# Two unread 512-column products at the turn of the second attention, and a new order of a few VectorE and ScalarE steps in the first attention and the feed-forward stages

## What is computed

```python
x = x + attn_a(layernorm(x), Wq, Wk, Wv, Wo)   # 16 heads of 16, masked softmax; 8 heads strided, 8 fixed
x = x + ffn(layernorm(x), w_gate, w_up, w_down) # 256 -> 704 -> 256
x = x + attn_b(layernorm(x), ...)               # 8 heads of 32
x = x + ffn(layernorm(x), ...)                  # the same weights again
```

```python
fid  = dots / (norm(qq) * norm(kq))            # a cosine, from 8 features per head
qw   = fid * (1.0 + 0.1 * sin(pi * fid))
aw   = 0.5 * qw + 0.5 * (Q @ K.T) / sqrt(32)
probs = softmax(aw); heads = probs @ V         # then Wo, a layernorm, a small middle net, a second layernorm
```

## Time and profile before

| | us |
|---|---|
| median of 3 runs | 3663.86 |
| lowest, highest | 3655.23, 3664.30 |
| the profiled execution, its own time | 3658.47 |
| its span | 3656.7 |
| mean granted clock of TensorE, share of full | 0.927 |

### The profile page before, as it was taken

How to read it: one execution, slowest core, us unless ns; L and a number is a source line. 1 busy time by engine, 2 the same in 40 slices (tenths; PEclk the granted TensorE clock), 3 DMA queues, 4 the chain that set the end, 5 groups by cost and what they waited for, 6 DMA issues and landing times. The chain is left out here.

```text
span 3656.7 us, 70567 instructions
## 1 busy us (share of the span) xinstructions
PE 3141.8 (86%) x24024; PEld 2441.3 (67%) x24024; DVE 2772.7 (76%) x7209; ACT 2187.4 (60%) x5360; POOL 1121.8 (31%) x664
## 2 busy tenths in 40 slices
PE   6899899899895899997588888888888886699998
PEld 4666666666664788887356565566665654688888
DVE  4676676676666788886488888888878887688887
ACT  4666667676672344433477777877777775344343
POOL 1000000000003455554233333444333333455554
PEclk9999999999996999999699999999999897899999
DMA  5344244244332100000334344443443443110000
GB/s 89 43 68 61 43 68 61 44 68 61 51 49 75 47 18 18 18 12 29 52 50 68 59 69 66 68 72 59 64 71 59 69 60 87 41 35 30 29 30 24
DMA packets 134183, 190.46 MB, mean 52 GB/s; under 512 B 15127, under 2 KB 81559, under 8 KB 133143
## 3 DMA queue, kind: packets, MB, share of 16 engines
q1 hardware_dynamic: 133830, 185.95, 29.9%
HBM read 45.65 MB, written 28.84 MB: 20 GB/s over the span
## 5 line engine op out<-in xcount | busy, mean ns | idle before, releaser
L407 ACT ACTIVATE a_probs<-a_probs,a_negmax 128x176 f32<-128x176 f32 (+4 forms) x1024 | 501.7, 490 | 331.6 <-DVE a_negmax L330 331.2
L330 DVE CUSTOM_DVE_ANT_0 a_probs<-a_mask,a_score 128x176 f32<-128x176 f32 (+4 forms) x1024 | 404.0, 400 | 222.4 <-PE a_score L481 90.2
L492 PE MATMUL a_turned<-ident,a_probs 128*128 128x128 f32 (+1 forms) x2176 | 427.7, 289 | 79.3 <-DVE a_pT L339 71.6
L1716 DVE CUSTOM_DVE_ANT_0 b_u<-b_u,b_score 128x512 f32<-128x512 f32 x512 | 340.4, 681 | 137.2 <-PE b_score L1971 134.8
L1841 ACT ACTIVATE b_u<-b_u,b_negmax 128x512 f32<-128x512 f32 x512 | 367.0, 717 | 113.6 <-DVE b_negmax L1716 112.2
L1245 PE MATMUL f_y_bank<-f_wdT,f_hqT 128*128 128x256 f32 x1536 | 374.7, 396 | 60.2 <-ACT f_hqT L1184 60.2
L1708 DVE SCALAR_TENSOR_TENSOR b_u<-b_u,b_score 128x1024 f32<-128x1024 f32 x256 | 310.1, 1215 | 94.2 <-ACT b_u L1834 91.7
L1245 PEld LDWEIGHTS f_y_bank<-f_wdT,f_hqT 128*128 128x128 f32 x1536 | 296.4, 197 | 108.5 <-issue 67.9
L1834 ACT ACTIVATE b_u<-b_score 128x1024 f32<-128x1024 f32 x256 | 262.3, 1025 | 163.3 <-PE b_score L1961 163.0
L1177 ACT ACTIVATE f_h_mag<-f_hu 128x704 f32<-128x704 f32 x128 | 101.4, 792 | 421.2 <-POOL f_hu L1060 421.2
L1980 PE MATMUL b_turned<-ident,b_u 128*128 128x128 f32 x2048 | 322.1, 282 | 24.7 <-DVE b_pT L1722 19.4
(11 more groups left out here) (236 smaller groups left out, 7160.5 us busy)
## 6 DMA issues: line engine op xcount, KB each, us to landing
b_stack<-b_part SPq DMA_DIRECT2D x192, 256.0 KB, 8.4
a_stack_q<-a_part SPq DMA_DIRECT2D x192, 128.0 KB, 4.3
a_stack_k<-a_part SPq DMA_DIRECT2D x192, 128.0 KB, 5.7
xs<-in_x_dram SPq DMA_DIRECT2D x16, 512.0 KB, 8.2
x_before_b<-xs SPq DMA_DIRECT2D x16, 512.0 KB, 2.9
b_xin<-x_before_b SPq DMA_DIRECT2D x16, 512.0 KB, 12.2
b_xres<-x_before_b SPq DMA_DIRECT2D x16, 512.0 KB, 3.8
x_after_b<-b_xres SPq DMA_DIRECT2D x16, 512.0 KB, 5.8
```

The source lines that it names most:

```text
L330: dve.tensor_tensor_reduce(out=probs[:, n % 2, j, 0:keys(n)], in0=mask_of(n), in1=score[j][:, 0:keys(n)], scale=-1.0, scalar=3.0e38, op0=A ...
L407: act.activation(probs[:, n % 2, j, 0:keys(n)], probs[:, n % 2, j, 0:keys(n)], ACT.Exp, bias=negmax[:, n, j:j + 1], scale=-1.0, accum_out= ...
L492: m = nc.tensor.transpose(turned[j % 2][0:rows, u, :], chunk(n, probs[:, n % 2, j, :], u), ident[:])
L1716: dve.tensor_tensor_reduce(out=u[:, n, j, :], in0=u[:, n, j, :], in1=score[:, j, :], scale=-0.05, scalar=3.0e38, op0=ALU.add, op1=ALU.min, ...
```

## The change

There are three edits, and no other.

1. First attention, VectorE: the side step of Q, K and R jobs moves from behind head 1 to behind head 2 (and its copy). V, y and input turns stay behind head 1, and ScalarE's order stays as it was.
2. Both feed-forward stages, ScalarE: `magnitude` moves behind `scalar_magnitude` (slot 0) and `scalar_standard` (slot 2).
3. Second attention, TensorE: `keep_busy` at (15, 1) and (15, 3), in the 16 bodies that have a next sequence: a product of the identity with 512 columns of a weight, written to the bank `out_acc`, which nobody reads before the next output product starts it anew.

```diff
-                        job = jobs.get(n - 1, "-") if j == 1 else "-"
+                        job = jobs.get(n - 1, "-")
+                        if j != (2 if job[0] in "QKR" else 1):
+                            continue
                         if job[0] == "R":
                             move_out(sequence(s, job), int(job[1]))
...
                         move_hidden(*behind(3))
-                    if behind(1):
-                        magnitude(*behind(1))
                     if n == 0 and has(s + 1):
                         front.scalar_magnitude(act, s + 1)
                     if n == 2 and has(s + 2):
                         front.scalar_standard(act, s + 2)
+                    if behind(1):
+                        magnitude(*behind(1))
...
+            def keep_busy(s):
+                wait(pe, s_o, 2 * s + 2)
+                mm(out_acc[:], ident[:], w["wq"][:].rearrange("p k n -> p (k n)"), start=True, stop=True)
...
                             do_side(s, jobs[n, j])
+                        if (n, j) in ((15, 1), (15, 3)) and has(s + 1):
+                            keep_busy(s)
```

## The result

The changed kernel takes 3560.57 us (median of 4 runs, 3560.35 to 3563.71), against 3660.21 us for the kernel before in its 4 runs (3655.23 to 3664.30). The ratio is 0.973, 95% interval 0.971 to 0.974: some 100 us off, where 148 were forecast (3512). The profiled execution took 3563.71 us, its span 3561.9, 94.8 less than before.

What follows compares the result with a forecast made beforehand. TensorE, through short waits and time at 1.2 GHz, was taken to bound the first two stages and the last; 84 + 39 + 27 = 150 us off 3658.5 gave 3508, stated as 3512 for a median; own range 3475 to 3545, wide 3450 to 3580.

Steps and rivals of the forecast that it cites:

- rival (a): First attention: the clock stays as it is, so its 48 us do not come, 3560 us; chance 12%.
- (b): Second attention: the two products do not hold the clock; 13 us slower instead of 27 off, 3552 us; chance 10%.
- (c): Feed-forward slot 0: head-of-line blocking, new wait 1.6 us, clock falls as before; stages gain 9 us, 3542; chance 12%.
- (d): First attention and feed-forward: waits close as far as they can, all the first attention's clock returns, 3450 us; chance 10%.
- the feed-forward's floor: Feed-forward: 29.40 us a sequence, seen without the L929 steps, taken as the floor of TensorE's own work.
- First attention, waits: 2.4 us a body: First attention: TensorE's closed waits give back 2.95 us a body, less 0.55, so 2.4; ends 0.5 and 4.6.
- 0.55 us taken: First attention: deduction per body for low parts coming later and holding the one `a_side` bank, as in job K0.
- First attention, clock: 3.2 us a body: First attention: nearly all the lost clock time comes back, 3.2 us a body at par; ends 0 and 5.5.
- Feed-forward: 39: Both feed-forward stages: 24 us from waits plus 17 from clock minus 2 at the ends, 39 off; ends 15 and 70.
- 1.75 us taken for how far VectorE could follow: Feed-forward: of the 2.03 us TensorE runs ahead, VectorE follows by 1.75, leaving a new slot 1 wait of 0.9.
- Second attention: 27: Second attention: two products hold the clock at the turn, 2.3 us off each, 27 in all; ends 40 off, 14 slower.
- a fall further on in the half may come instead (3 us off): Second attention, softmax half: 3 us deducted from the 34 us gain because the clock may fall later instead.

Runs made afterwards that it cites:

- hold_a: Kernel before, VectorE's order unchanged, plus two unread 512-column products in each of 15 first-attention bodies, in slots 13 and 15: 3628.92 us, ratio 0.991.
- std_only: Changed kernel with the feed-forward magnitude ahead of the input's step again in slot 0, behind it only in slot 2: 3533.29 us.
- fill_only: Kernel before plus one unread product ahead of N0 (first softmax-half side job with 16-column products), none at the turn: 3653.05 us, ratio 0.997.
- keep_only: Kernel before with the third edit alone, the two unread products at the second attention's turn: 3660.43 us over 10 runs, ratio 1.000.
- fill_two: Changed kernel plus two unread products in the softmax half, one ahead of N0 and one behind a score in slot 5: 3522.56 us.
- fill_n0: Changed kernel plus one more unread 512-column product ahead of N0, the first softmax-half side job with 16-column products: 3522.14 us.

## Why the prediction was right, and where it was short

**The bound and the direction.** Right: TensorE's waits and its clock were what the edits could take, and two of three stages gave it. The time stands inside the wide range (3450 to 3580) and outside the forecast's own (3475 to 3545): 100 us came of 148. It is within 1 us of rival (a)'s 3560, and that is luck, for the clock gain of the first attention did come. What happened has something of two others: the second attention's gain was lost as in (b), but not by a turn that did not hold the clock, and slot 0 of the feed-forward queued as in (c), but without its fall of the clock. One sum of the rivals is off: (d) takes 25 us for the feed-forward's floor, and the end given above, 70 against 39, is 31.

**First attention, waits: 2.4 us a body, measured 1.8.** The gaps closed nearly as worked out. With Q0 and K0 early the closed waits are 65.2 - 62.6 = 2.6, for 2.95 in the sum. The price of the one `a_side` bank was mis-sized: 0.55 us taken, 0.8 measured (63.4 - 62.6). K0 in slot 8 was named as the job that would be late, and the row that would show it is the wait at L462.

**First attention, clock: 3.2 us a body, measured 2.4.** The falls went altogether, as told. The clock time lost was 43 us by the trace's clock records and not 47, since 0.955 reads as 0.95 in the earlier trace rows. The size came from the two bodies of the earlier trace rows, which differ by 2.5 us; the prediction took the rest of the low clock to cost in proportion and so went "at par" with the lost clock time. The low stretches of the two, 6.8 us in one and 3.4 in the other:

```profile
507.10:513.90 6.80, 6.80 (x35) 4.29 (x35) 2.12 (x12) 3.30 (x14) 0.00 (x0) 0.50 0.00 0
585.60:589.00 3.40, 3.40 (x29) 2.47 (x27) 2.64 (x12) 2.50 (x11) 0.00 (x0) 0.50 0.00 0
```

`hold_a` shows a body without any: 65.2 us, where this straight line had given 63.6, my expectation for it. The line went through two bodies alone. Of the 14 steady bodies of the kernel before, measured between VectorE's first copies, six have 3.4 us at the low clock and take 66.4 us in the mean (66.0 to 66.8), six have 6.8 and take 68.2 (67.5 to 68.7), two have 10.2 and take 69.2; the eleven of `hold_a` without any take 65.3 by the same marks. So 3.4 us at the low clock cost 1.0 to 1.8 us, 1.3 in the mean, and not 2.5. In `hold_a` itself they cost 1.5 (66.8 us). Why the price differs from body to body is not shown; TensorE is busy all through both stretches above.

**Rival (a) and the rule on turns.** Rightly turned down. The transposes of the first attention lie closer together and the clock is at 1.00 over 887 us. The Trainium skill ("TensorE: Matmul & The Clock Gate", Part 4: PE-mode transpose) says that a transpose does not count as busy for the clock in the way of other products. By that rule the prediction had said that the clock gain would not come, and it came. That does not refute the rule by itself: the transposes into `a_turned` are 358 of TensorE's 818 busy us there, other products stand between them, and no run here has transposes alone.

**Feed-forward: 39, measured 27 in this pair of profiles, 33 by the mean of all.** In steady sequences the waits give 31.56 - 31.11 = 0.45 us, not 0.9: slot 3 gives 1.71 (forecast 1.83), slot 1 takes 1.26 (forecast 0.9, end 1.6). The term that was mis-sized is the 1.75 us taken for how far VectorE could follow ("at least by 1.03, at most by all"): it came out near 1.4, if the new wait is worked out from 1.26 instead of 0.9 as there, which is an estimate. 26 x 0.45 = 12 us, for 24. The clock gives 11 falls x 1.7 = 18.5, for 17 told, and 24 against the 14 falls of the other profiles. The sequence that had no L929 step before pays 1.74 us in each stage, 3.5 for 2 told. Together 27, or 33 with 14 falls. The floor of 29.40 us was not TensorE's alone: in that sequence VectorE is busy 26.02 us instead of 28.6. `std_only` shows that half of the edit was a loss: rival (c)'s queueing in slot 0, without its fall of the clock. The prediction had put the price there, and left slot 0 in the edit.

**Second attention: 27, measured 0.** The turn was right in each mark: 1.00, B0 in 1.88 us, VectorE's wait 0.23, and 2.4 us gained for 2.3. Wrong was the term "a fall further on in the half may come instead (3 us off)". It came in the third interval in 13 of 14 bodies, and 1.5 us a body went there and in the sixth, some 22 us and not 3 in all. A further 1.0 us a body (15 us) goes in the second interval, where ScalarE has no idle time left; the prediction had named no engine as next. With a product ahead of N0 the bodies take 78.5 us in the mean, and the stage is 37 us shorter than the 1430 of the kernels without the edit: the third and sixth interval are 4.4 and 4.5 us, and of the second's 1.0 some 0.8 stay lost. Not all of the 37 are the turn's: 13 come with the product at N0 alone (`fill_only`), which also removes falls that the kernel before had. The other 24 or 25 are what the two products at the turn are worth once the later falls are held, near the 27 forecast. So the mechanism held, and its cover lay 10 us too short.

**The additions' cost.** None can be seen, as told: `keep_only` is not slower in 10 runs, and the first scores wait 0.41 us for cosine terms, not for the product.

**Still open.** Why the fall at 27.8 us went with that at 10.6: it stood some 17 us behind it in each of the nine bodies that had both. It does not need the earlier one: four bodies of the kernel before have a fall at 26.9 to 28.0 us and none at 10 to 12, and with the product at N0 alone 13 of 14 bodies have none at either place. The product at N0 may have changed what TensorE does there or only when; `fill_two` cannot tell these apart, since its product found almost nothing to hold.

## What to carry to other kernels

Price a fall of the clock by a body that has none, or make one with an unread product in a free bank: it measures the clock's share by itself, and costs nothing where the engine waits. When a fall is held in one place, look at the next places with waits and small products before counting the gain; here three products together gave 38 us, two of them alone 0 and the third alone 8 to 13. Compare stages over all profiles at hand and not in one pair: here the pair was 5 us too high in one stage and 6 too low in another. When a step is moved past one that waits for a slow engine, split the edit by slot: one slot may gain what another loses.

## What the runs showed of the hardware that was not expected

- A single product of 512 columns (L1912 in `fill_n0`: the next product starts 0.86 us later) at one place of a 79 us body removes two low stretches 17 us apart, in 13 of 14 bodies.
- The clock fell at places where TensorE had stood for 0.6 and 1.0 us, beside eight products of 16 columns, and did not fall where it had stood 1.28 us between products of 512 columns. It is no fixed outcome: two bodies of `keep_only`, with the same code, have no fall at the first place.
- The falls fall into a pattern: 8 of 14 bodies of the changed kernel have low stretches at nearly the same three offsets from the first score (9.4 to 10.8, 26.5 to 27.9 and 64.1 to 65.4 us), and six of them a period of 81.8 to 81.9 us, where the bodies of the kernel before vary from 78.8 to 82.9 (between the first maxima). The third stretch, in the cosine half, costs some 0.3 us.
